# A recommendation tower on one core: sample products on four groups of 32 output rows instead of two of 64, remainders in halves, one store per part, and another order of the late work

## What is computed

```python
e = jnp.stack([tbl_0[ids[:, 0]], ..., tbl_25[ids[:, 25]]], axis=1)   # 512 samples, 26 tables, rows of 128
all_emb = concatenate([r_bottom_output[:, None, :], e], axis=1)      # 27 features of 128 per sample
gram = einsum('bfd,bgd->bfg', all_emb, all_emb)
z = gram[:, triu_i, triu_j]                                          # 351 products of pairs per sample
h = maximum(concatenate([z, r_bottom_output], axis=1) @ W_top1 + b_top1, 0)   # 479 -> 512
h = maximum(h @ W_top2 + b_top2, 0)                                  # 512 -> 256
y = h @ W_top3                                                       # 256 -> 1
```

## Time and profile before

| quantity | value |
|---|---|
| median of 3 runs | 120.17 us |
| profiled execution | 119.29 us |
| its span | 117.5 us |
| around the span | 1.8 us |
| PE busy | 108.8 us (93%) |
| DVE busy | 70.5 us (60%) |
| ACT busy | 63.8 us (54%) |
| POOL busy | 71.2 us (61%) |
| instructions in the trace | 2578 |

### The profile page before, as it was taken

One profiled execution on the slowest core, in us unless ns is written; L12 is line 12 of the kernel. 1 busy time (PEld: TensorE's weight loads), 2 busy tenths in 40 slices (PEclk: granted clock), 3 DMA queues, 4 the chain that ended last, 5 costly groups with the idle time before them and its releaser, 6 DMA issues.

```text
span 117.5 us, 2578 instructions
## 1 busy us (share of the span) xinstructions
PE 108.8 (93%) x1004; PEld 87.5 (74%) x1004; DVE 70.5 (60%) x75; ACT 63.8 (54%) x87; POOL 71.2 (61%) x73
## 2 busy tenths in 40 slices
PE   5899999999999999999998990999799999999892
PEld 5778676776868776776667980899799799797890
DVE  1669999999999999999952640024242422121021
ACT  3395899999999969687505342222334123212111
POOL 2667868777777777787867767767777002030000
PEclk9999999999999999999999998559999999999999
DMA  3999999999879879932111238427545612710000
GB/s 50 283 246 259 258 268 259 262 280 204 246 200 268 239 175 288 267 109 73 43 46 50 66 65 155 108 69 131 113 106 110 112 49 41 107 44 0 23 0 1
DMA packets 19914, 16.67 MB, mean 142 GB/s; under 512 B 13785, under 2 KB 15701, under 8 KB 19902
## 3 DMA queue, kind: packets, MB, share of 16 engines
q1 hardware_dynamic: 16707, 12.03, 42.3%
q0 software_dynamic: 2160, 4.30, 14.1%
q10 hardware_dynamic: 1035, 0.18, 1.0%
HBM read 15.01 MB, written 1.49 MB: 140 GB/s over the span
## 4 chain that ended last, share of the span: by engine, by line
POOL 45%; PE 32%; issue 12%; DMA 6%; POOLq 1%; ACT 1%; DVE 1%; ACTq 0%; DVEq 0%
POOL mixed_sb L336 45%; PE banks L443 10%; PE banks L481 9%; PE banks L488 6%; PE banks L475 3%; PE banks L425 3%; DMA mixed_sb<-in_mixed_table,mixed_rows_sb 2%; DMA starts_sb<-in_starts 2%; DMA pairs<-products_dram 1%; POOLq L340 1%; PE banks L495 1%; ACT hidden L666 1%; DVE hidden L608 0%; ACTq L322 0%; DVE mixed_rows_sb L644 0%
## 5 line engine op out<-in xcount | busy, mean ns | idle before, releaser
L336 POOL DMA_INDIRECT mixed_sb<-in_mixed_table,mixed_rows_sb x64 | 68.6, 1072 | 21.4 <-issue 19.2
L620 DVE TENSOR_SCALAR one_hot<-banks,starts_sb 125x1024 fp32r<-125x1024 f32 x34 | 41.7, 1276 | 1.6 <-PE banks L392 1.4
L413 PE MATMUL banks<-one_hot,high 125*128 125x512 f32 x68 | 28.9, 426 | 0.1
L415 PE MATMUL banks<-one_hot,low 125*128 125x512 f32 x68 | 27.0, 397 | 0.0
L413 PEld LDWEIGHTS banks<-one_hot,high 125*128 125x128 f32 x68 | 13.0, 192 | 8.6 <-issue 3.2
L443 PE MATMUL banks<-turned 128*56 128x52 f32 x512 | 17.3, 232 | 1.1 <-issue 0.7
L443 PEld LDWEIGHTS banks<-turned 128*56 128x56 f32 x512 | 16.1, 148 | 2.7 <-issue 2.4
L584 DVE COPY products<-banks 120x416 f32<-120x416 f32 (+1 forms) x9 | 7.4, 826 | 15.9 <-PE banks L443 13.6
L695 ACT COPY turned<-banks 128x512 f32<-128x512 f32 x10 | 10.7, 1068 | 8.1 <-PE banks L415 8.1
L666 ACT ACTIVATE hidden<-banks,b_sb 128x128 f32<-128x128 f32 x12 | 4.4, 368 | 19.4 <-PE banks L481 11.8
L415 PEld LDWEIGHTS banks<-one_hot,low 125*128 125x128 f32 x68 | 13.1, 192 | 2.1
(11 more groups left out here) (33 smaller groups left out, 88.3 us busy)
## 6 DMA issues: line engine op xcount, KB each, us to landing
raw<-in_tbl SPq DMA_DIRECT2D x6, 448.0 KB
lookup_ids_sb<-in_lookup_ids SPq DMA_DIRECT2D x10, 256.0 KB, 7.1
raw<-in_tbl SPq DMA_DIRECT2D x4, 560.0 KB
products_dram<-products SPq DMA_DIRECT2D x14, 91.0 KB
mixed_sb<-in_mixed_table,mixed_rows_sb POOLq DMA_INDIRECT x64, 6.4
pairs<-products_dram SPq DMA_DIRECT2D x15, 39.0 KB
w_sb<-in_w SPq DMA_DIRECT2D x2, 256.0 KB
w_sb<-in_w SPq DMA_DIRECT2D x1, 512.0 KB, 13.2
```

The lines of the kernel that those rows point to most:

```text
L336: pool.indirect_dma_start(mixed_sb[:, n, :], None, mixed_table, bass.IndirectOffsetOnAxis(ap=mixed_rows_sb[:, n:n + 1], axis=0),).then_inc ...
L413: pe.matmul(lookup_ps[:, i % 2, :], high[0:TABLE_PARTS, i % 2, c, :], columns, start=(c == 0), stop=False)
L415: last = pe.matmul(lookup_ps[:, i % 2, :], low[0:TABLE_PARTS, i % 2, c, :], columns, start=False, stop=(c == CHUNKS_OF[i] - 1))
L620: dve.tensor_scalar(one_hot[0:TABLE_PARTS, n % ONE_HOT_RING:n % ONE_HOT_RING + ONCE, :], banks[0:TABLE_PARTS, first:last + 1, :], float(-c ...
```

## The change

Six edits come together.

1. A product matmul takes one sample: 28 columns of weights, 26 moving columns. The four samples of a quad go to PSUM partitions 0, 32, 64 and 96. There are twice as many matmuls, a block is 32 matmuls and 64 records; nothing across samples is computed. The clearing of the banks and PE's wait for it are gone. `keep` copies 124 partitions x 208 elements instead of 120 x 416.
2. The remainder of a table is made in two halves, and between and behind them stands the one-hot of a single chunk in place of one pair. Table 0 is also rounded in two halves, and PE waits for the half that a chunk needs.
3. A part is stored by one transfer, 124 rows of 3328 bytes, issued by SP. POOL and ACT store nothing.
4. A part is loaded by seven transfers as before, in pieces of 384 bytes (four of them) and of 128 bytes (three); `pairs` lies in another order in SBUF, and the rows of W_top1 are ordered to match.
5. The turn of block i-1, not i-2, stands behind lookup i, and the late order is another.
6. Two warm-up matmuls instead of four stand ahead of the first lookup.

```diff
-WARM_UPS = (8, 4)
+WARM_UPS = (8, 2)
-LATE_ORDER = "mmmm tm tm tm mm mm tmm oo tom o tom ooo to tmm oo ooo ooooooo"
+LATE_ORDER = "mmt mmmmmt mmmmmt oooooom toooom ooo ttoo tmmm oooooo"
...
+def halves_of(i):
+
+    return [slice(0, CHUNKS_OF[i] // 2), slice(CHUNKS_OF[i] // 2, CHUNKS_OF[i])]
...
         if i >= 2:
-            turn_up_to(i - 2)
-    turn_up_to(len(LOOKUP) - 2)
+            turn_up_to(i - 1)
+    turn_up_to(len(LOOKUP) - 1)
...
-            for j in samples:
+            eng.dma_start(bass.AP(products_dram.tensor, p * PRODUCT_ROWS * ROW, [[ROW, PRODUCT_ROWS], [1, ROW]]),
+                          products[:, p % 2, :, :].rearrange("r g q -> r (g q)")).then_inc(stored[p], 16)
...
+                    pairs[part:part + rows, p, :, chunk:chunk + chunks, :].rearrange("r j c q -> r j (c q)"),
+                    bass.AP(products_dram.tensor, start + row * QUADS,
+                            [[step * QUADS, rows], [SAMPLE_ROWS * ROW, QUAD], [1, chunks * QUADS]])
...
                 for c in range(CHUNKS_OF[i]):
+                    if c == 0:
+                        pe.wait_ge(high_set, highs(i, 0))
+                        pe.wait_ge(low_set, 2 * i + 1)
+                    elif c == halves_of(i)[1].start:
+                        pe.wait_ge(high_set, highs(i))
+                        pe.wait_ge(low_set, 2 * i + 2)
...
-                    for h in range(HALVES):
-                        samples = slice(h * PAIR, (h + 1) * PAIR)
-                        rows = slice(h * HALF_START, h * HALF_START + PAIR * SLOTS)
-                        last = pe.matmul(product_ps[rows, b % len(PRODUCT_BANKS), k, 0:PAIR * OTHERS],
-                                         turned[:, t, q, samples, :].rearrange("p j f -> p (j f)"),
-                                         turned[:, t, q, samples, 1:FEATURES], start=True, stop=True)
+                    for j in range(QUAD):
+                        last = pe.matmul(product_ps[sample_rows(j), b % len(PRODUCT_BANKS), k, 0:OTHERS],
+                                         turned[:, t, q, j, :], turned[:, t, q, j, 1:FEATURES],
+                                         start=True, stop=True)
...
-            pe.wait_ge(banks_cleared, 1)
...
-                make_one_hot(i, 0)
-
+                make_one_hot(i, 0, ONCE)
                 dve.wait_ge(table_in[i], 16 * 2)
-                dve.wait_ge(high_set, i + 1)
...
+                for half, chunks in enumerate(halves_of(i)):
+
+                    dve.wait_ge(high_set, highs(i, half))
+                    dve.tensor_tensor(low[0:TABLE_PARTS, i % 2, chunks, :],
+                                      raw[0:TABLE_PARTS, i % RAW_RING, chunks, :],
+                                      high[0:TABLE_PARTS, i % 2, chunks, :].bitcast(F32), ALU.subtract
+                                      ).then_inc(low_set, 1)
+                    make_one_hot(i, ONCE + half, 1)
+                for c in range(ONCE + 2, VECTOR_CHUNKS_OF[i], ONCE):
+                    make_one_hot(i, c, ONCE)
...
-            dve.memset(banks[UNUSED_ROWS, PRODUCT_BANKS[0]:PRODUCT_BANKS[-1] + 1, :], 0.0
-                       ).then_inc(banks_cleared, 1)
...
-                    if n == BLOCKS - 1:
-                        store_part(act, LAST_PART, ACT_STORES, stored[LAST_PART])
```

More of the change, by code:

```diff
@@ L87 @@
 SPARE = P - PER_CHUNK * OTHERS
-PAIR_LOADS = [(0, OTHERS * i, i, OTHERS, 3, PER_CHUNK, FEATURES) for i in range(PER_CHUNK)]
+PAIR_LOADS = [(0, OTHERS * i, 3 * i, OTHERS, 3, 1, FEATURES) for i in range(PER_CHUNK)]
 PAIR_LOADS += [(0, PER_CHUNK * OTHERS, SPAN - 1, SPARE, 1, 0, FEATURES),
@@ L103, with highs @@
 ID_ROWS, ID_COLUMNS = len(LOOKUP) + 1, BATCH + 2 * len(LOOKUP)
+def halves_of(i):
+    return [slice(0, CHUNKS_OF[i] // 2), slice(CHUNKS_OF[i] // 2, CHUNKS_OF[i])]
+def highs(i, half=1):
+    return i + 1 + (half if i == 0 else 1)
 def tile_of(b):
@@ L298, in sample_rows, with store_part, load_part @@
         def sample_rows(j):
-            first = j // PAIR * HALF_START + j % PAIR * SLOTS
-            return slice(first, first + SLOTS)
-        def store_part(eng, p, samples, signal):
+            return slice(j * SAMPLE_ROWS, j * SAMPLE_ROWS + SLOTS)
+        def store_part(eng, p):
             for k, keeper in enumerate(kept):
                 eng.wait_ge(keeper, kept_by(k, PARTS[p][1]))
-            t, quads = tile_and_quads(p)
-            n = quads.stop - quads.start
-            start = ROWS * columns_of(p).start
-            for j in samples:
-                eng.dma_start(
[L311 to L325, removed]
+            eng.dma_start(bass.AP(products_dram.tensor, p * PRODUCT_ROWS * ROW, [[ROW, PRODUCT_ROWS], [1, ROW]]),
+                          products[:, p % 2, :, :].rearrange("r g q -> r (g q)")).then_inc(stored[p], 16)
+        def load_part(eng, p, loads, signal):
+            eng.wait_ge(stored[p], 16)
+            start = p * PRODUCT_ROWS * ROW
+            for chunk, part, row, rows, chunks, chunk_step, step in loads:
+                assert chunks == 1 or chunk_step == 1
+                eng.dma_start(
+                    pairs[part:part + rows, p, :, chunk:chunk + chunks, :].rearrange("r j c q -> r j (c q)"),
+                    bass.AP(products_dram.tensor, start + row * QUADS,
+                            [[step * QUADS, rows], [SAMPLE_ROWS * ROW, QUAD], [1, chunks * QUADS]])
+                ).then_inc(signal, 16)
         @block.gpsimd
@@ L480, in add_pairs @@
                 for c, rows in enumerate(CHUNK_ROWS):
-                    last = pe.matmul(out(n), w1_sb[0:rows, c, h * P:(h + 1) * P], pairs[0:rows, c, columns_of(p)],
-                                     start=False, stop=(c == PAIR_CHUNKS - 1))
+                    last = pe.matmul(out(n).rearrange("h (j q) -> h j q", j=QUAD), w1_sb[0:rows, c, h * P:(h + 1) * P],
+                                     pairs[0:rows, p, :, c, :], start=False, stop=(c == PAIR_CHUNKS - 1))
                 return last
@@ L580, in keep @@
             if t >= 2 and tile_of(b - 2) < t:
-                eng.wait_ge(stored[t - 2], 16 * len(hardware_stores(t - 2)))
+                eng.wait_ge(stored[t - 2], 16)
             quads = quads_of(b)
-            copy(products[:, t % 2, :, :, quads].rearrange("p j g q -> p q (j g)"),
-                 product_ps[0:HALF_END, b % len(PRODUCT_BANKS), 0:quads.stop - quads.start, 0:PAIR * OTHERS]
+            copy(products[:, t % 2, :, quads].rearrange("p g q -> p q g"),
+                 product_ps[0:PRODUCT_ROWS, b % len(PRODUCT_BANKS), 0:quads.stop - quads.start, 0:OTHERS]
                  ).then_inc(kept[which], 1)
@@ L672, in round_table @@
                     act.wait_ge(chunk_used, FIRST_CHUNK[i - 1])
-                act.copy(high[0:TABLE_PARTS, i % 2, 0:CHUNKS_OF[i], :],
-                         raw[0:TABLE_PARTS, i % RAW_RING, 0:CHUNKS_OF[i], :]).then_inc(high_set, 1)
+                for chunks in halves_of(i) if i == 0 else [slice(0, CHUNKS_OF[i])]:
+                    act.copy(high[0:TABLE_PARTS, i % 2, chunks, :],
+                             raw[0:TABLE_PARTS, i % RAW_RING, chunks, :]).then_inc(high_set, 1)
             def make_one_hots(i):
```

57 lines of the change are left out of this document (20 added, 37 removed).

## The result

The change made the kernel slower: 132.33 us median of 4 runs (132.2 to 133.62) against 121.03 before (118.61 to 123.32), ratio 1.111, 95% interval 1.094 to 1.128. The forecast was 115.7 us, range 112.0 to 121.5. The profiled run has a span of 130.4 us against 117.5.

A forecast was written before the change was run, and what follows sets the result against it. Bounds: DVE and PE, both full in the lookups; then PE in program order, waiting for POOL's late gathers. 117.5 + 1.3 - 2.7 - 2.6 + 2.0 - 2.1 + 0.3 + 0.2 = 113.9, with 1.8 around the span 115.7 us; range 112.0 to 121.5.

The forecast's parts named there:

- Lookups (+1.3): Lookup stage: one more remainder and one-hot instruction per table on DVE, partly under PE; +1.3 us, bounds -0.4 and +2.1.
- gathers (-2.7): POOL's gathers: halved remainders hold them less, so PE's 2.69 us wait for block 11's gather goes; -2.7 us.
- Store and loads (+0.3 and +0.2): Part stores and loads: one transfer saves three issues, about 3.3 us; +0.3 before the first output, +0.2 for the last part.
- Products (+2.0): Product matmuls on PE: a block takes 0.95 us instead of 0.83, over 16 full blocks; +2.0 us.
- Clock (-2.6): PE behind the lookups: without the gather wait the stretch at 1.2 GHz goes; -2.6 us, range 0 to -2.6.
- Order (-2.1): PE's late steps: wait before block 12, relus and lone product groups saved, a new 0.25 us wait added; -2.1 us.
- price per record: Products: each record costs 25.9 ns to issue whatever its columns, a block 1.66 us, products +13.5; 127.2 us, chance 0.23.
- The gathers stay late: POOL's gathers: halves hold POOL as long in sum, PE waits 1.8 us, clock may fall; 120.1 us, chance 0.17.

The follow-up runs named there:

- the run on two groups: Changed kernel with products on two groups of 64 rows again (32 records per block) and each part stored by four transfers of 28 rows: 115.85 us, ratio 0.962.
- 121.96: Changed kernel with one edit, each part stored by two transfers, rows 0 to 111 and 112 to 123, instead of one of 124: 121.96 us, ratio 1.011.
- 114.4: Changed kernel with products on two groups, four stores of 28 rows, halved remainders kept, and the order of the kernel before: 114.4 us, ratio 0.966.

## Why the prediction was wrong, step by step

- **Lookups (+1.3) and gathers (-2.7)**: right by their rows: the lookups end at 63.8 against 63.7, the gathers take 61.6 us against "under 64", and PE's wait is gone.
- **Store and loads (+0.3 and +0.2)**: the step that failed most. I took "3.3 us; bounds 0.9 and 5.8" from the issues that one transfer saves, and measured 8.1 to 8.9. I priced the queue that issues and held the transfer itself for constant, though one of 403 KB takes the place of four of 91, and its 124 rows get few engines. The +0.3 stood for a wait before the first output; that wait did not come, because the slow products gave the loads time (in the run on two groups it came, with 1.70 us). The waits came at the third part (1.46 us) and at the last (5.45 us), and ACT's loads, forecast near 104, were issued at 117.2. The step's worth is 10.4 us by the medians (132.33 against 121.96; some 12 by the ratios to before, 1.111 and 1.011); of this PE's two waits for pairs give 6.9 and the half clock behind the second 2.2. The code of before holds a hint, which I passed by: it loads each table of 125 rows as 112 and 13.
- **Products (+2.0)**: the second step. The bounds 0.83 and 1.66 for a block were both prices of a record by itself, streamed or issued. By itself a block is cheaper than either (128 records in 1.51 us at 107.08, 0.76 a block); what counts in a run of blocks is the pace at which instructions come, 3.5 to 4.6 us from burst to burst of 256, so 1.7 us a block and more. This pace is nearly the same at both clocks (3.9 us at full, 3.5 and 4.0 at half), so the split of a block's price by the two clocks could not show it. The two-group products take 3.52 us for 128 records, the same pace, so the trace of before stands just at this limit and shows no stop. In the runs the four groups cost 6.1 us (121.96 against 115.85), in the kernel before 3.6.
- **Clock (-2.6)**: not gained here, though the run on two groups shows full clock from 12 us on. The wait for the gather went, but PE's stops took its place, and behind the wait for the last pairs the clock fell once more: 17.06 and 6.83 us at 1.2 GHz instead of 6.83 alone.
- **Order (-2.1)**: I added it to the gathers' -2.7, and in the runs on two groups the two do not add up: with whole remainders the order gives 2.0 us, with halves nothing (115.85 against 114.4). The traces say why: the new order takes 1.4 us off PE's busy time either way (106.8 to 105.4 and 105.7 to 104.3 us) and brings a wait of 2.02 or 1.70 us before the first output, and it spares the waits for gathers (2.2 us) only where the halves have not done so. Without the products' +2.0 my sum says 113.7 for the run on two groups, which took 115.85.
- **The rivals**: "price per record" had the sign, and its mark (blocks 1.3 us or more apart) was met, but not its reason: by itself a record on four groups costs 11.8 ns (1.51 us / 128), 28 cycles at 2.4 GHz, and not 25.9. The Trainium skill's rule of some 60 cycles a matmul ("TensorEngine Tiling (Array Packing)", "Instruction Overhead"), which the prediction cites, does not hold across four groups by this number. (The rival's +13.5 us is 13.3, 16 x 0.83, which changes no chance.) "The gathers stay late" fell. That a store could get slower was in no rival.

So 115.85 + 6.1 + 10.4 = 132.3 us. This splits one difference in the order in which the two faults were taken out, the store first; it is no check of the two sizes.

## What to carry to other kernels

When transfers are merged, ask over how many DMA engines the merged one runs: cut or pad its outer rows to a multiple of 16 (112 and 12, or 128), and look at the DMA share of a stretch inside it. When many small matmuls replace fewer, price them three ways: array, clock, and instructions per microsecond; a long run of them that uses 256 in under 3.5 us stopped here, a block or two between outputs hardly did. Gains that remove the same wait must not be added up.

## What the runs showed of the hardware

- The row count of a transfer alone moved the time from a store of 403 to 416 KB to its loads between 2.4 and 12.7 us.
- PE's instruction supply: 128 records with their loads per fetch of 16 KB, and stops of 1 to 2 us when these are used up in under 2. The Trainium skill, "Runtime: NRT & Kernel Launch", section "Instruction fetch mechanics", has blocks of 256 instructions fetched ahead and their cost mostly hidden; the size agrees, the hiding does not hold here. In the kernel after a fetch begins 1.1 to 2.2 us into a burst, takes 0.9 to 1.3 us, and PE goes on 1.3 to 1.5 us behind its end, which makes the 3.5 us and more. Why a fetch does not begin earlier, and whether other transfers delay it, was not tried.
- Records on four groups of 32 rows followed each other at 11.8 ns, against 27.5 for a record of 56 columns on two groups (3.52 us / 128), with half of its columns in each; that they overlap more is inferred from this.
